# Eight-head attention layer: order of the row and column sends, the unit exponential and the unit sums

## What is computed

```python
h = (x @ W).reshape(n, heads, out_c)
al_s = jnp.einsum('nhc,hc->nh', h, a_src)
al_d = jnp.einsum('nhc,hc->nh', h, a_dst)
e = jax.nn.leaky_relu(al_s[src] + al_d[dst], NEG_SLOPE)
m = jax.ops.segment_max(e, dst, num_segments=n)
ex = jnp.exp(e - m[dst])
z = jax.ops.segment_sum(ex, dst, num_segments=n)
alpha = ex / (z[dst] + 1e-16)
msg = h[src] * alpha[:, :, None]
out = jax.ops.segment_sum(msg, dst, num_segments=n)
...
h = gat_layer(x, W1, a_src1, a_dst1, b1, src, dst, heads=8, out_c=96, concat=True)
h = jax.nn.elu(h)
```

## Time and profile before

| what | value |
|---|---|
| median of 3 runs | 1486.38 us (1481.84 to 1487.33) |
| profiled execution, its own time | 1486.36 us |
| its span | 1484.4 us |
| mean granted TensorE clock, share of full speed | 0.968 |
| PE busy | 1389.2 us, 94% of the span |
| DVE busy | 770.3 us, 52% |
| ACT busy | 446.5 us, 30% |
| POOL busy | 546.8 us, 37% |
| head loop of the eight-head layer | about 1297 to 1398 us of the span |

### The profile page before, as it was taken

One profiled execution on the slowest core, in us unless ns is written; L12 is line 12 of the kernel. 1 busy time (PEld: TensorE's weight loads), 2 busy tenths in 40 slices (PEclk: granted clock), 3 DMA queues, 4 the chain that ended last, 5 costly groups with the idle time before them and its releaser, 6 DMA issues.

```text
span 1484.4 us, 22402 instructions
## 1 busy us (share of the span) xinstructions
PE 1389.2 (94%) x7674; PEld 1287.8 (87%) x7674; DVE 770.3 (52%) x1843; ACT 446.5 (30%) x953; POOL 546.8 (37%) x626
## 2 busy tenths in 40 slices
PE   5999999999999999999999899889989999787797
PEld 3677999999999999999999889889978977677784
DVE  7876755134544374672323344554464615587644
ACT  2555421111100101110101221344574434556531
POOL 8001243242425344353433332043325545345530
PEclk9999999999999999999999999999999999976899
DMA  3111111122343152341211211122002211200001
GB/s 113 54 32 34 33 43 54 33 64 64 107 128 113 37 144 64 96 137 45 64 42 55 62 56 33 39 86 76 27 22 79 70 43 43 69 1 1 1 11 52
DMA packets 57783, 86.47 MB, mean 58 GB/s; under 512 B 6448, under 2 KB 54439, under 8 KB 57564
## 3 DMA queue, kind: packets, MB, share of 16 engines
q1 hardware_dynamic: 45184, 65.82, 15.1%
q10 hardware_dynamic: 12504, 19.36, 4.5%
HBM read 83.24 MB, written 1.92 MB: 57 GB/s over the span
## 4 chain that ended last, share of the span: by engine, by line
PE 76%; DVE 12%; ACT 3%; POOL 3%; issue 3%; DMA 2%; DVEq 0%; ACTq 0%; SPq 0%; POOLq 0%
PE psum L2438 13%; PE psum L2442 13%; PE psum L2441 13%; PE psum L2455 8%; PE psum L2458 8%; PE psum L2916 4%; PE psum L2578 2%; DVE max_scratch L2143 2%; PE psum L2503 2%; PE psum L2966 2%; POOL w_lo L911 2%; PE psum L2817 1%; PE psum L2821 1%; PE psum L2822 1%; PE psum L2427 1%
## 5 line engine op out<-in xcount | busy, mean ns | idle before, releaser
L2438 PE MATMUL psum<-w_lo,xT_hi 128*125 128x384 f32 (+5 forms) x1140 | 390.1, 342 | 7.0 <-DVE x_nat L1869 2.5
L2442 PE MATMUL psum<-w_hi,xT_hi 128*125 128x384 f32 (+5 forms) x1140 | 385.4, 338 | 0.0
L2441 PE MATMUL psum<-w_hi,xT_lo 128*125 128x384 f32 (+5 forms) x1140 | 385.3, 338 | 0.0
L898 POOL CAST w_hi<-w_raw 128x384 fp32r<-128x384 f32 x190 | 104.4, 550 | 591.1 <-PE psum L2442 483.9
L2438 PEld LDWEIGHTS psum<-w_lo,xT_hi 128*125 128x125 f32 (+1 forms) x1140 | 213.3, 187 | 10.5 <-POOL w_lo L911 3.4
L1073 ACT ACTIVATE h_hi<-psum 125x384 fp32r<-125x384 f32 (+1 forms) x120 | 59.0, 492 | 532.3 <-PE psum L2442 527.9
L1711 DVE TENSOR_TENSOR h_lo<-psum,h_hi 125x384 fp32r<-125x384 f32 (+1 forms) x120 | 66.9, 558 | 285.7 <-ACT h_hi L1073 284.4
L2441 PEld LDWEIGHTS psum<-w_hi,xT_lo 128*125 128x125 f32 (+1 forms) x1140 | 213.8, 188 | 0.4
L2442 PEld LDWEIGHTS psum<-w_hi,xT_hi 128*125 128x125 f32 (+1 forms) x1140 | 213.1, 187 | 0.0
L900 POOL TENSOR_TENSOR w_lo<-w_raw,w_hi 128x384 fp32r<-128x384 f32 x190 | 200.9, 1058 | 15.2
L2455 PE MATMUL psum<-h_lo,adjacency 125*125 125x384 f32 (+3 forms) x600 | 203.6, 339 | 2.1 <-issue 1.9
(11 more groups left out here) (348 smaller groups left out, 2226.4 us busy)
## 6 DMA issues: line engine op xcount, KB each, us to landing
w_raw<-weights_dram SPq DMA_DIRECT2D x296, 192.0 KB, 2.4
score_w_raw<-weights_dram ACTq DMA_DIRECT2D x58, 192.0 KB, 2.9
x_nat<-x_dram SPq DMA_DIRECT2D x1, 1875.0 KB
x_residual<-x_dram SPq DMA_DIRECT2D x1, 1875.0 KB
score_a_rows<-L_gnn_a_src_dram ACTq DMA_DIRECT2D x8, 192.0 KB, 3.5
score_a_rows<-L_gnn_a_dst_dram ACTq DMA_DIRECT2D x8, 192.0 KB, 4.8
out_dram<-x_residual SPq DMA_DIRECT2D x4, 375.0 KB
rgcn_bias<-rgcn_bias_dram SPq DMA_DIRECT2D x1, 1125.0 KB
```

The lines of the kernel that those rows point to most:

```text
L898: nc.gpsimd.tensor_copy(mem.wh[:, slot, :], mem.raw[:, raw_slot, :]).then_inc(w_hi_ready, 1)
L2438: ins = nc.tensor.matmul(o, h, wl, start=(j == 0), stop=False, skip_group_check=True)
L2441: nc.tensor.matmul(o, l, wh, start=False, stop=False, skip_group_check=True)
L2442: ins = nc.tensor.matmul(o, h, wh, start=False, stop=stop and j == k - 1, skip_group_check=True)
```

## The change

On TensorE the first tile's products no longer stand ahead of the two sends: `send_row(h + 2)` and `send_columns(h + 1)` are issued first, and then all 25 products of head h. On ScalarE `elu_exp(h - 1)` is issued behind the exponentials of head h+1 instead of ahead of them. On GpSimd the loop body is cut in two: the bias of unit h stays where it was, and the clip and the sum are those of unit h-1, so that unit 6 is finished behind the loop. No instruction is added or taken away but for joined repetitions; no DMA is moved.

```diff
--- before.py
+++ after.py
@@ -1003,16 +1003,26 @@
                     pool.wait_ge(tile_exp, scored(Q2, h, k))
                     nc.gpsimd.tensor_tensor(t, t, counts, ALU.mult).then_inc(late_ready, 1)
 
-            for h in range(LAST):
+            def unit_bias(h):
+
+                pool.wait_ge(part_read, Q2.unit0 + h + 1)
+                nc.gpsimd.tensor_tensor(strip(h), strip(h), bias_strip(h), ALU.add).then_inc(elu_in, 1)
+
+            def unit_sum(h):
+
                 e, t = mem.elu[0:BP, h % 2, :, :], strip(h)
-                late_products(h + 1)
-                pool.wait_ge(part_read, Q2.unit0 + h + 1)
-                nc.gpsimd.tensor_tensor(t, t, bias_strip(h), ALU.add).then_inc(elu_in, 1)
                 pool.wait_ge(elu_out, h + 1)
                 nc.gpsimd.tensor_scalar(e, e, 1.0, -1.0, ALU.min, ALU.add).then_inc(elu_low, 1)
                 pool.wait_ge(elu_low, h + 1)
                 pool.wait_ge(elu_pos, h + 1)
                 nc.gpsimd.tensor_tensor(t, t, e, ALU.add).then_inc(layer_ready, 1)
+
+            for h in range(LAST):
+                late_products(h + 1)
+                unit_bias(h)
+                if h:
+                    unit_sum(h - 1)
+            unit_sum(LAST - 1)
             split_to(NCHUNKS)
 
             pool.wait_ge(params_loaded, 16 * 9)
@@ -1508,8 +1518,6 @@
                     head_read(h - 1)
                 if h + 1 < HEADS3:
                     keep_flat(Q2, h + 1)
-                if h:
-                    elu_exp(h - 1)
                 if h + 1 < HEADS3:
                     for k in range(NB - LATE):
                         source_exp(Q2, h + 1, k)
@@ -1520,6 +1528,8 @@
                         if k + 1 < NB:
                             source_below(h + 1, k + 1)
                         source_exp_below(h + 1, k)
+                if h:
+                    elu_exp(h - 1)
                 split_hi(min(chunks_split[0] + 3, Q2.end + AHEAD))
             elu_exp(LAST)
             for n in range(NB, 2 * NB):
@@ -3093,12 +3103,11 @@
                 if h == LAST:
                     for n in range(NB):
                         turn_x3(n)
-                sum_head(h, 0, 1)
                 if h + 2 < HEADS3:
                     send_row(Q2, h + 2)
                 if h < LAST:
                     send_columns(Q2, h + 1)
-                sum_head(h, 1, NB)
+                sum_head(h, 0, NB)
                 if h + 2 < HEADS3:
                     turn_columns(Q2, h + 2)
```

## The result

The kernel after takes 1476.06 us (median of five runs, 1475.54 to 1480.23), against 1483.2 us for five runs of the kernel before beside it (1481.84 to 1487.33). The ratio is 0.9948, 95% interval 0.9932 to 0.9964: 7.1 us faster, at the edge of the 0.5% that the prediction set. Two later comparisons of the same two kernels gave 0.9940 (0.9917 to 0.9964) and 0.9933 (0.9912 to 0.9954), by the medians 9.9 and 10.5 us. Of all runs one lay in a slower state, 1548.6 us at a granted clock of 0.84 against about 0.97 in the others: the median of TensorE's part alone counts it in, the ratio there does not.

What follows compares the result with a forecast made beforehand. VectorE's rounds in the eight-head layer's loop were taken as bound by its wait for TensorE's row. Gains and losses of 9.7-2.2-1.1-1.1 = 5.3 us gave 1481.1 us; own range 1479 to 1485, stated range 1478 to 1490.

Steps and rivals of the forecast that it cites:

- Part 1: Head loop: sends ahead of sums remove VectorE's wait for the row; 9.7 of 11.9 us had, VectorE's round 11.9 us.
- I take half, 2.2 us: Heads 1 to 5: TensorE's lower clock gives back half of 4.3 us; the ends are 0 and 4.3.
- The ring: TensorE's round of sends, 50 sums, column turning and ScalarE's copy: 8.6 us near full clock, 15.0 at the lower.
- The first two waits: VectorE's waits at heads 0 and 1, 0.86 and 1.33 us, counted as no gain because sums end later.
- So the sum against it needs no correction: Base time: the profiled execution, 1486.36 us, lay 0.02 us below the median of three runs, so was used uncorrected.
- The own range, 1479 to 1485: Whole kernel: narrowed from gains of 9.7 us with all ends good and 1.2 with all bad.
- Parts 2 and 3: End of the loop: ScalarE's uncovered pair at head 6 costs 1.1 us, GpSimd's later units another 1.1.
- The rule weighed: VectorE's column arithmetic: only two-input GpSimd work stalls it, one 1.20 us operation as before; one-input work is not charged.
- The fourth rival: Five rounds: GpSimd's one-input work holds VectorE's column arithmetic up to 1.81 us each, 9.1 in all; 1488.0 us, chance 0.04.
- TensorE at the lower clock: Head loop: TensorE becomes the bound, 15.0 us a round instead of 14.06; 1494.2 us, chance 0.12.
- The clock stays up: Head loop: TensorE's ring is 8.6 us and nothing of the 9.7 is given back; 1478.9 us, chance 0.12.
- The other two: Head loop: row still late, 1488.6 us, chance 0.14; or GpSimd's one-input work holds VectorE, 1488.0 us, chance 0.04.

Runs made afterwards that it cites:

- TensorE's part alone: The kernel before with only the sends moved ahead of all the sums; 1475.68 us, ratio 0.994 to the kernel before.
- the first profile: The profiled execution of the unchanged kernel after from its first five runs, the longest of them; 1480.23 us, five rounds of 62.60 us.
- the second and third profiles: The kernel after run again twice, unchanged; medians 1475.22 and 1476.04 us, five rounds of 59.91 and 59.93 us.
- the first pair: The first profiled executions of the kernels before and after, 1486.36 and 1480.23 us; heads 1 to 5 took 70.25 and 62.60 us.
- spare products: The kernel after with ten unread products added on TensorE behind heads 1, 3 and 5; 1475.91 us, ratio 0.9949.
- pair back: The kernel after with ScalarE's exponential and positive part of unit 4 back ahead of head 6's exponentials; 1476.27 us.
- old end: The kernel after, GpSimd's clip ahead of the bias for units 0 to 3, old ScalarE and GpSimd order for units 4 to 6; 1473.5, then 1475.1 us.

## Why the prediction was wrong

- **Part 1, the mechanism, was right.** The row is there when VectorE has done its two tiles, the wait of the maxima falls from 11.9 us to nothing inside the loop (0.5 in the first profile), and VectorE's round is 11.93 us against the predicted 11.9. TensorE's part alone gives it.
- **The step that failed is the size of "I take half, 2.2 us".** In the rounds of the second and third profiles VectorE waited for TensorE nowhere, so the term was nothing; in the first profile it was 1.46 us. That the rounds of the first pair gain 70.25-62.60 = 7.65 us, as 9.7-2.2 = 7.5 said, is luck: 1.46 us given back and 2.0 us more hold stand there against 1.1 us of head 1's wait that went too. The term was too large for two reasons. The ring was drawn on a straight line from 8.6 to 15.0 us by the share of time at the lower level, but a share of time has to weigh the rates: at a clock of 0.71 that is 1/(0.58/15.0+0.42/8.6) = 11.4 us and not 12.3, and over the five rounds 2.8 and not 4.3. The ring at 0.71 measured in the second profile needs 11.6 us, less than the round of 11.93. And each round's excess over 11.9 was added up, while a late send lies beside VectorE's two tiles: the ring of 14.22 us, 2.29 over 11.93, cost 0.94+0.26.
- **The first two waits, which "I count at nothing", were mostly had.** Head 0 takes 22.80 us instead of 23.75 in the second and third profile of after. In the first it takes 23.84, as the prediction argued; over the nine profiles with the sends ahead of the sums it goes with the clock of that stretch (22.8 at 0.70 in five, 23.8 at 0.64 in three, 25.35 at 0.60). Head 1's wait, 1.33 us, left 0.26 in the first profile and nothing in the others, though in the second a hold of 1.25 us instead of 0.67 took part of it back.
- **Put together**, for the middle one of each kernel's three profiles (the first of before, the second of after): 9.7 for the other four waits, 0.95 and 1.33 for the first two, nothing given back, 5.5-4.5 = 1.0 us more hold, 1.85 us lost at the end. That is 9.1 us, and the stretch from the first score to the transposes gains 116.23-106.79 = 9.4.
- **"So the sum against it needs no correction" failed.** The profiled execution lay on the median of the three runs shown, but the median of the five was 1483.2. More important, the five rounds of the three profiled executions of before differ by up to 3.8 us, 3.3 of it hold, so that one execution can't stand for them. In the first comparison the two misses add up: the base was 3.2 us above the median of its five runs, the gain 1.8 too small. In the later comparisons, with before at 1485.15 and 1486.53, nearly the whole miss is the gain: 9.9 and 10.5 us for 5.3.
- **The own range, 1479 to 1485, was cut by judgement** ("as these ends hardly meet"). The good end, 9.7, was about what happened: in two of the three profiles of after nothing was given back and head 0's wait was had as well. Both hang on TensorE's clock, but in different stretches: with the spare products and with TensorE's part alone head 0's wait was lost, and the rounds still gave back only 0.25 us.
- **Parts 2 and 3 were right in sum and parts.** Predicted 1.1+1.1 = 2.2; in the first pair the stretch to the transposes grows by 24.49-22.23 = 2.26, of which about 0.99 is the pair (pair back) and the other 1.27 is put down to GpSimd's queue. In the other profiles of after the stretch is 24.04 and 24.08, in those of before 22.21 and 23.43, so the loss lies anywhere from 0.6 to 2.3 us; "old end" did not show that it can be had back.
- **The rule weighed was half right on either side.** The price was one hold of 1.0 us in each round as before. In fact the kernel before pays 0.2 to 0.9 us a round on average, by chance of timing, and the kernel after pays 1.06 in each undisturbed round, since the bias now always meets the column arithmetic and the clip follows it. That is TensorE's part, not GpSimd's new order: TensorE's part alone has 5.7 us of hold. The clip holds a column operation only in about its first 0.6 us (1350.30 to 1350.81, for a clip that starts at 1350.19), not for its 1.8. The Trainium skill ("SBUF — State Buffer", "SBUF: two separate sides") has GpSimd and a two-input VectorE operation lock each other out for a whole instruction; the bias rows agree, the clip rows agree in that there is a hold and not in its length. The fourth rival, 1.81 us a round, was five times too dear (0.34).
- **The rivals.** TensorE at the lower clock did not become the bound: the longest round is 12.96 us, at a clock of 0.52. "The clock stays up" came out closest in time (1478.9), but not by its reason: the clock did fall, and falling to 0.71 cost nothing. The other two did not come about.

## What to carry to other kernels

Take a second and third profile before a sum of a few microseconds is set against one execution, and look at which rows differ between them: here the rounds of the kernel before differ by 3.8 us, 3.3 of it hold, and in one round of each that was whether a small operation began 0.02 us ahead of another engine's or 0.04 us behind it. Where an engine's ring is longer than the round only at a low clock, weigh the two levels by their rates, charge what goes beyond the slack at the place where the two meet, and let the next round repay, rather than adding up the excess of each round. And do not cut a range because its ends seem unlikely to meet: here most of the good ends did.

## What the runs showed of the hardware

- A GpSimd TENSOR_TENSOR of 1.2 us holds VectorE's 5- and 10-column operations on SBUF until it ends: 0.17 us becomes up to 1.20. VectorE's maxima (0.81 us) and scores (0.87 and 3.19 us in a row), which read PSUM, kept their lengths beside GpSimd's products and sums. A product of two SBUF tiles did not, at the end of the loop of the kernel after beside GpSimd's last products (0.80 us elsewhere), and GpSimd's product that began beside it, at 1386.55, took 2.09 us (1.51 elsewhere), so that the hold goes both ways:

```profile
1385.37 1.90 DVE L2209 SCALAR_TENSOR_TENSOR score_tiles<-score_tiles,counts_all 125x625 f32<-125x625 f32 x1
1386.55 2.09 POOL L1004 TENSOR_TENSOR score_tiles<-score_tiles,par0b 125x625 f32<-125x625 f32 x1
```

- A GpSimd TENSOR_SCALAR of 1.8 us holds such an operation in its first 0.6 us, counted from its recorded start; in its middle 0.17 us stays 0.17. Once a CAST late in it took 0.50 us (1345.56, above). Why only there stays open.
- The same program runs through the same loop at different clocks in different executions (0.52 to 0.97 by rounds in one, 0.71 to 0.86 in another), and the 13 executions of the table reach it at 1281.5 to 1287.5 us. What sets it was not tried.
